# Last stage of a fused kernel: scatters ahead of low parts, both tile tables spread over tiles, the last expert's low parts shared between two engines, expert numbers read early, the last product in halves

## The chip, the cores and the metric

One of the eight cores of a Trainium2 chip runs the whole program. The metric is the time on the device in microseconds, the median of several executions. Five engines run their own instruction streams and meet at semaphores: PE (matmuls and transposes), DVE and ACT (vector work), POOL (vector work and the indirect DMAs, which it issues itself) and SP (the other DMAs).

## What is computed

The input x is 4096 tokens (2 sequences of 2048) of 512 features. Four layers are each added to it: cross attention, a quantised feed-forward, a masked cross attention, and at the end a layer of experts. The change is in the last one alone:

```python
def _L1_ffn_ref(x, Wg, bg, We, be):          # x: the layer norm of the residual
    probs = jax.nn.softmax(x @ Wg + bg, axis=-1)         # 512 probabilities a token
    idx = jnp.argmax(probs, axis=-1)
    p = jnp.take_along_axis(probs, idx[..., None], axis=-1)[..., 0]
    e_idx = idx % We.shape[0]                             # 8 experts
    h = jax.nn.relu(jnp.einsum('bsd,edf->besf', x, We) + be[None, :, None, :])
    onehot = jax.nn.one_hot(e_idx, We.shape[0], dtype=x.dtype)
    out = jnp.einsum('besf,bse->bsf', h, onehot) * p[..., None]
    return out
...
x = x + _L1_ffn_ref(_layernorm(x, axis=-1), L1_ffn_Wg, L1_ffn_bg, L1_ffn_We, L1_ffn_be)
```

So each token needs the product with one of eight 512x512 matrices, that of the expert its argmax names, then bias, relu, the factor p, and its own residual row.

## The kernel before

The expert stage is the class ExpertStage. It walks over tiles of 128 tokens with one running number t. Tiles 0 to 31 are gate tiles, in the order of the tokens, and four of them make a group (0 to 7). Tiles 32 to 70 are the 39 product tiles, j = t - 32, of rows that have been sorted by expert. The gate tiles 0 to 3 belong to the end of the attention stage; from t = 4 on every engine runs a loop `rest` of its own over t, and the order of the calls in that loop is the order on the engine.

A tile passes through the engines like this. ACT's `norm(t)` (L2516) writes the normalised tile. PE's `turn(t)` transposes it (four matmuls, L2766). ACT's `take_hi(t)` (L2523) copies the transposed tile out rounded, and DVE's `take_lo(t)` (L2587) takes what the rounding left. PE multiplies both parts with the two parts of a weight: three matmuls for each of four 128-row pieces k. In gate tiles this is `logits(t)` (L2776 to L2778); in product tiles `product(j)` (L2819 to L2821), whose expert is read from a table into a register. In its iteration t PE does `turn(t + 1)`, then the matmuls of t. Of what it multiplies the low parts of the expert weights are made by POOL (`weights_low`, L2468) from the loaded weights and from their high parts, which ACT casts (`weights_high`, L2535). The high parts of expert e >= 2 are written over the residual rows of group e - 2, so they wait until those rows have been scattered.

In gate tiles DVE finds the largest logit and its index (`top`, L2596 to L2601), ACT sums the exponentials (L2529). After each group DVE makes the one-hots (`hot`, L2606 to L2613), PE ranks the rows within their experts by small matmuls (`rank_rows`, L2789 to L2799), DVE turns the ranks into places (`places`, L2618 to L2628), and POOL scatters the four tiles of residual rows to these places in DRAM (`scatter_rows`, L2477).

Each expert's region in DRAM is rounded to whole tiles, in two steps. After six groups (EARLY = 6) an early count tells of 17 tiles (FULL_TILES) that are certainly full, and after all eight a late count places the other 22 (REST_TILES). Each step is a chain of small DVE instructions: `tile_count` (L2633 to L2641), `tile_ends` (L2646 to L2652), `early_ends` or `late_ends`, and `tile_table` (L2662 to L2675), which writes `tile_expert` and `tile_row`. The early chain stands at t = 25, 26 and 27, the late one at t = 34, 35 and 36. `no_row` (t = 33) and `rows_behind` (t = 34) prepare filler rows, which SP writes behind each expert's last row and at the end (nine DMAs), the first ahead of load 8 and one behind each of loads 8 to 15.

SP loads the sorted rows of product tile j into one of eight buffers (`load`, L2418). Load 0 waits for the early table and six scattered groups, load 4 for seven groups, load 17 for the late table, all groups and all filler rows; from load 8 on each waits until tile j - 8 is finished. In product tiles DVE adds the bias (`add_bias`, L2713, which first reads the expert's number), and in `finish` takes relu and factor (L2719) and adds the residual (L2721) into one of four y buffers; POOL scatters this to the output (`scatter_out`, L2484). The next use of the buffer waits for that DMA.

In POOL's loop two low parts of expert e stand ahead of the scatter of group e - 1 and two behind it, and waits on `out_full` and `hot_ready` hold the low parts back to set times. Of expert 7, pieces 0 and 1 wait until PE has done tile 28, pieces 2 and 3 until DVE has made the last one-hots, in its iteration t = 32. Product 0 waits for the low parts of expert 7 piece by piece.

## Time and profile before

| what | value |
|---|---|
| runs (three) | 1486.5, 1483.89, 1485.26 us; median 1485.26 |
| profiled execution | 1482.94 us |
| its span | 1481.1 us, so 1.8 us lie around it |
| mean granted clock of TensorE | 0.988 |
| busy share of the span | PE 96%, DVE 81%, ACT 58%, POOL 35% |
| expert stage, tiles 4 to 70 | transposes of tile 4 at 1234.24, last matmul near 1469.5 |
| DVE busy, 1370 to 1463 us | 73.6 of 93 us |
| last indirect DMA issued | 1472.60 |

A line of a timeline gives start and duration in microseconds, engine, line of the kernel, operation, what is written from what, and how many instructions the line merges. In square brackets stands how long the engine had been idle before it, and which instruction released it. Matmul durations overlap, so the distance between starts is what counts. PEclk is the clock that TensorE was granted, as a share of 2.4 GHz.

### The profile page before, as it was taken

Reading aid. Unit: us, or ns where it says so; the run is one execution under the profiler, and the core shown is the slowest. Engines: PE = TensorE matmul, PEld = TensorE weight load, DVE = VectorE, ACT = ScalarE, POOL = GpSimd, SP = SyncE. Lnnn points to the kernel's source line nnn. Section 1 sums busy time; section 2 is a strip of 40 time slices with the busy share of each in tenths; the row PEclk is TensorE's granted clock in tenths of the full one; section 3 lists DMA queues with packets and bytes.
Section 4 is the critical chain, followed back from the end, with each engine's and each line's share of the span. In section 5 each row is a group of like instructions: output and inputs, shape, how many; then the busy total and the mean of one; then the engine's idle time right before and its main releaser. Section 6 shows DMA issues by size and latency. Waiting matters only on the chain. (4 is left out here: it accounts for less than half of the span.)

```text
span 1481.1 us, 30113 instructions
## 1 busy us (share of the span) xinstructions
PE 1420.4 (96%) x10457; PEld 1065.1 (72%) x10478; DVE 1198.1 (81%) x2580; ACT 864.1 (58%) x2056; POOL 523.6 (35%) x507
## 2 busy tenths in 40 slices
PE   7999999999999999899998999999999989998996
PEld 5777777777777777644443467888888877776885
DVE  6778787887878765699988968999999986787775
ACT  2544444444444444655548747999999876773432
POOL 0122222222222222200004646655656655664333
PEclk9999999999999999999999999999999999999998
DMA  8511111110111102235507610000000025226641
GB/s 302 185 47 46 46 46 46 46 42 8 37 39 40 46 8 79 47 107 185 184 16 287 246 42 2 4 2 3 3 4 4 4 87 209 98 94 200 193 152 57
DMA packets 68658, 122.03 MB, mean 82 GB/s; under 512 B 30398, under 2 KB 36926, under 8 KB 67008
## 3 DMA queue, kind: packets, MB, share of 16 engines
q1 hardware_dynamic: 62864, 103.71, 20.7%
q0 software_dynamic: 5680, 16.85, 2.9%
q8 instruction: 66, 1.08, 0.3%
q14 instruction: 48, 0.39, 0.1%
HBM read 77.46 MB, written 39.80 MB: 79 GB/s over the span
## 5 line engine op out<-in xcount | busy, mean ns | idle before, releaser
L1835 ACT ACTIVATE c_probs<-c_score,c_minus_top 128x128 f32<-128x128 f32 x512 | 181.2, 381 | 27.9 <-DVE c_minus_top L1981 25.7
L1778 POOL TENSOR_TENSOR c_probs<-c_probs,c_recip 128x512 f32<-128x512 f32 x128 | 140.8, 1103 | 131.2 <-DVE c_recip L1991 127.5
L700 POOL TENSOR_TENSOR a_attn_lo_parts<-a_attn,a_attn_hi_parts 128x512 fp32r<-128x512 f32 x64 | 80.6, 1291 | 200.5 <-ACT a_attn_hi_parts L762 200.5
L758 ACT COPY a_attn<-a_pv_ps 128x512 f32<-128x512 f32 x64 | 36.6, 572 | 145.3 <-PE a_pv_ps L1068 145.3
L1451 POOL TENSOR_TENSOR xres<-xres,b_delta 128x512 f32<-128x512 f32 x24 | 48.3, 2028 | 196.9 <-DVE b_delta L1508 196.9
L1835 ACT ACTIVATION_READ_ACCUMULATOR c_probs<-c_score,c_minus_top 128x1 f32 x512 | 112.8, 220 | 0.0
L430 PE MATMUL a_bank<-a_x_hi_parts,a_wq_hi 128*128 128x256 f32 x512 | 106.5, 289 | 0.3 <-PEq L445 0.3
L696 POOL TENSOR_TENSOR a_x_lo_parts<-a_x_full,a_x_hi_parts 128x512 fp32r<-128x512 f32 x30 | 38.0, 1289 | 192.9 <-ACT a_x_hi_parts L733 192.9
L430 PE MATMUL a_bank<-a_x_lo_parts,a_wq_hi 128*128 128x256 f32 x512 | 102.4, 281 | 0.0
L430 PE MATMUL a_bank<-a_x_hi_parts,a_wq_lo 128*128 128x256 f32 x512 | 102.3, 281 | 0.0
L727 ACT ACTIVATE a_x_full<-a_bank,a_shift,a_gain 128x256 f32<-128x256 f32 x60 | 30.2, 555 | 119.4 <-PE a_bank L422 119.4
L1036 PE MATMUL a_bank<-a_wo_hi,a_attn_hi_parts 128*128 128x512 f32 x248 | 99.4, 401 | 0.0
L1038 PE MATMUL a_bank<-a_wo_hi,a_attn_lo_parts 128*128 128x512 f32 x248 | 98.1, 396 | 0.0
L1037 PE MATMUL a_bank<-a_wo_lo,a_attn_hi_parts 128*128 128x512 f32 x248 | 98.0, 395 | 0.0
L2523 ACT CAST d_xT_hi<-c_score 128x512 fp32r<-128x512 f32 x67 | 39.3, 587 | 97.9 <-PE c_score L2766 92.1
L1304 ACT ACTIVATE b_silu<-b_gate,ahead_scale 128x512 f32<-128x512 f32 x88 | 60.2, 684 | 61.7 <-PE b_gate L1380 61.1
L742 ACT ACTIVATE a_probs<-a_score_ps 128x1024 f32<-128x1024 f32 x64 | 65.6, 1025 | 41.2 <-PE a_score_ps L1053 41.2
L1975 DVE COPY_PREDICATED_SCALAR c_score<-c_masks,c_tiny 128x512 f32 (+1 forms) x96 | 89.1, 928 | 0.0
L1380 PE MATMUL b_up<-b_xT,ahead_upT 128*128 128x512 bf16 x342 | 88.5, 379 | 0.3
L1380 PE MATMUL b_gate<-b_xT,ahead_gateT 128*128 128x512 bf16 x340 | 88.2, 379 | 0.4
L430 PEld LDWEIGHTS a_bank<-a_x_hi_parts,a_wq_hi 128*128 128x128 f32 x512 | 78.3, 188 | 14.2 <-issue 6.3
L1981 DVE TENSOR_REDUCE c_minus_top<-c_score 128x4 f32<-128x512 f32 (+1 forms) x96 | 83.4, 869 | 3.3
(352 smaller groups left out, 4244.3 us busy)
## 6 DMA issues: line engine op xcount, KB each, us to landing
hidden<-b_hidden SPq DMA_DIRECT2D x5, 2816.0 KB, 8.3
b_hidden<-hidden SPq DMA_DIRECT2D x5, 2816.0 KB, 11.4
xres<-in_x SPq DMA_DIRECT2D x8, 1024.0 KB, 14.4
d_we<-in_we SPq DMA_DIRECT2D x8, 1024.0 KB, 6.5
xres<-in_w_gate_up SPq DMA_DIRECT2D x7, 1024.0 KB, 5.3
d_got<-rows SPq DMA_DIRECT2D x20, 258.0 KB, 2.8
xres<-rows SPq DMA_DIRECT2D x19, 258.0 KB, 2.6
a_rot<-in_rot SPq DMA_DIRECT2D x16, 256.0 KB, 3.0
```

Source lines behind the costliest of these rows:

```text
L430: last = nc.tensor.matmul(out[:, i, :], w[:, k, cols], x[:, k, :], start=(j == 0 and i == 0), stop=(j == len(products) - 1 and i == 1))
L700: nc.gpsimd.tensor_tensor(of_spread(attn_lo, g), of_spread(attn, g), of_spread(attn_hi, g), ALU.subtract).then_inc(attn_lo_ready, 1)
L742: nc.scalar.activation(buf, score_ps[:, p % 2], ACT.Tanh, scale=1.0 / (DH0 ** 0.5 * GROK)).then_inc(capped, 1)
L1036: nc.tensor.matmul(out, hi, w_hi, start=first, stop=False)
L1037: nc.tensor.matmul(out, hi, w_lo, start=False, stop=False)
L1038: return nc.tensor.matmul(out, lo, w_hi, start=False, stop=last)
L1304: nc.scalar.activation(silu[:, u % RING, :], gate_ps[:, u % RING, :], ACT.Silu, scale=gate_scale[:, i:i + 1]).then_inc(silu_ready, 1)
L1380: last = nc.tensor.matmul(ps[:, u % RING, :], w[:, k, i * P:(i + 1) * P], xT[:, n % 2, k, :], start=(k == 0), stop=(k == KB - 1))
L1778: nc.gpsimd.tensor_tensor(part, part, recip[:, t % 2, heads].unsqueeze(2).to_broadcast([P, QUADS, KEYS]), ALU.mult).then_inc(scaled, 1)
L1835: last = nc.scalar.activation(probs[:, t, at, :], score_ps[:, h, g, :], ACT.Exp, bias=minus_top[:, h, g:g + 1], accum_out=total[:, t, at:a ...
L1975: ch.step(nc.vector.copy_predicated(part, masks[:, j, t, :].unsqueeze(1).to_broadcast(shape), tiny[:].unsqueeze(2).to_broadcast(shape)))
L1981: nc.vector.tensor_reduce(minus_top[:, PIECES[i]].rearrange("p h g -> p (h g)"), part, AX.X, ALU.max, negate=True).then_inc(top_ready, 1)
```

## The change

In POOL's loop the scatter of group e - 1 comes first and all four low parts of expert e behind it; of expert 7 POOL makes only pieces 0 and 1, then scatters group 6. Group 7 is scattered two tiles at a time behind the first two outputs. DVE makes pieces 2 and 3 of expert 7 at t = 31 (`last_low`). ACT's casts for group 2 stand at t = 10 and 11 (two each) in place of 9, 10, 11; those of expert 7 at t = 29 and 30. The early chain has fewer steps, and its first table step stands a tile earlier; of `early_ends` four steps go to t = 34. The late chain is spread over t = 34 to 39. DVE reads an expert's number at the end of the tile before. SP writes the nine filler rows at loads 11 to 14 (FILL = 11). The last product, its bias and its finish are done in two halves of 256 columns.

```diff
+        FILL = G + 3
+        LAST_SLOT, HALVES = SLOT_TILES - 1, (slice(0, D // 2), slice(D // 2, D))
         def pieces(t):
+            if t // TPC == 2:
+                return {0: (), 1: (), 2: (0, 1), 3: (2, 3)}[t % TPC]
             return {0: (), 1: (0, 1), 2: (2,), 3: (3,)}[t % TPC]
...
-                sp.wait_ge(no_row_set, 2)
-                sp.dma_start(io["rows"][NO_ROW:NO_ROW + P, :], no_token[:]).then_inc(filled, 16)
-                sp.wait_ge(behind_ready, 1)
                 for j in range(G, SLOT_TILES):
                     load(j)
-                    if j - G < EXPERTS:
-                        first = sp.value_load(behind_u[0:1, j - G:j - G + 1], min_val=0, max_val=NO_ROW - P)
-                        sp.dma_start(io["rows"][bass.ds(first, P), :], no_token[:]).then_inc(filled, 16)
+                    if j == FILL:
+                        sp.wait_ge(no_row_set, 2)
+                        sp.dma_start(io["rows"][NO_ROW:NO_ROW + P, :], no_token[:]).then_inc(filled, 16)
+                        sp.wait_ge(behind_ready, 1)
+                    for e in range(2 * (j - FILL), 2 * (j - FILL) + 2):
+                        if 0 <= e < EXPERTS:
+                            first = sp.value_load(behind_u[0:1, e:e + 1], min_val=0, max_val=NO_ROW - P)
+                            sp.dma_start(io["rows"][bass.ds(first, P), :], no_token[:]).then_inc(filled, 16)
...
             def weights_low(e, k):
                 pool.wait_ge(we_hi_ready, KB * e + k + 1)
-                if e >= 1 and k < 2:
+                if e >= 1 and k < 2 and e != EARLY:
                     pool.wait_ge(out_full, done(TPC * e))
-                elif e >= 1:
+                elif 1 <= e < EXPERTS - 1:
                     pool.wait_ge(hot_ready, e + 1)
...
-                for e in range(1, EXPERTS):
-                    for k in range(2):
+                for e in range(1, EXPERTS - 1):
+                    scatter_rows(e - 1)
+                    for k in range(KB):
                         weights_low(e, k)
-                    scatter_rows(e - 1)
-                    for k in range(2, KB):
-                        weights_low(e, k)
-                scatter_rows(GROUPS - 1)
+                for k in range(2):
+                    weights_low(EXPERTS - 1, k)
+                scatter_rows(GROUPS - 2)
                 for j in range(SLOT_TILES):
                     scatter_out(j)
+                    if j < 2:
+                        scatter_rows(GROUPS - 1, range(2 * j, 2 * j + 2))
...
                     if t < GATES:
-                        for k in pieces(t):
+                        for k in pieces(t) if t < GATES - 2 else ((2, 3), ())[t - GATES + 2]:
                             weights_high(t // TPC, k)
...
-                ch.step(nc.vector.tensor_copy(counts[:], counted(i)))
-                ch.wait()
-                ch.step(nc.vector.tensor_scalar(whole[:], counts[:], float(add), None, ALU.add))
-                ch.wait()
-                ch.step(nc.vector.tensor_copy(whole_i[:], whole[:]))
+                ch.step(nc.vector.tensor_scalar(whole_i[:], counted(i), float(add), None, ALU.add))
...
+            def last_low():
+                for k in range(2, KB):
+                    at = EXPERTS - 1, k
+                    dve.wait_ge(we_hi_ready, KB * EXPERTS - KB + k + 1)
+                    nc.vector.tensor_tensor(we_lo[:, at[0], k], we[:, at[0], k], we_hi[:, at[0], k], ALU.subtract).then_inc(constants, 1)
...
                     if t > GATES:
-                        add_bias(t - GATES - 1)
+                        add_bias(t - GATES - 1, number)
...
                         finish(t - GATES - 1)
+                    if t >= GATES:
+                        number = expert_number(t - GATES)
...
                     if t == TPC * EARLY + 2:
                         early_ends()
+                        tile_passed(FULL_TILES)
                     if t == TPC * EARLY + 3:
-                        tile_table(0, FULL_TILES)
-                    if t == GATES + 1:
+                        tile_experts(0, FULL_TILES)
+                        tile_rows(0, FULL_TILES)
+                    if t == GATES - 1:
+                        last_low()
+                    if t == GATES + 2:
+                        early_taken()
+                    if t == GATES + 3:
                         no_row()
-                    if t == GATES + 2:
+                    if t == GATES + 4:
                         tile_count(1, P - 1)
                         rows_behind()
-                    if t == GATES + 3:
+                    if t == GATES + 5:
                         late_ends()
-                    if t == GATES + 4:
-                        tile_table(FULL_TILES, REST_TILES)
-                add_bias(SLOT_TILES - 1)
-                finish(SLOT_TILES - 1)
+                    if t == GATES + 6:
+                        tile_passed(REST_TILES)
+                        tile_experts(FULL_TILES, REST_TILES)
+                    if t == GATES + 7:
+                        tile_rows(FULL_TILES, REST_TILES)
+                for half in range(len(HALVES)):
+                    add_bias(LAST_SLOT, number, half)
+                    finish(LAST_SLOT, half)
...
+                for half, cols in enumerate(HALVES if j == LAST_SLOT else (slice(0, D),)):
+                    if half == 1:
+                        out = logit_place(t + 1)
+                        pe.wait_ge(y_used, j - RING + 2)
+                    for k in range(KB):
+                        if j == 0 and k >= 2:
+                            pe.wait_ge(constants, CONSTANTS + k - 1)
+                        elif j == 0:
+                            pe.wait_ge(we_lo_ready, KB * (EXPERTS - 1) + k + 1)
```

Left out are: `tile_passed`, `tile_experts` and `tile_rows`, which are `tile_table` in three parts, with its last casts folded into the instruction before (9 instructions become 7); `early_taken`, the last four steps of `early_ends`; `rows_behind`, one instruction in place of two; and `add_bias`, `finish` and the matmuls with the columns of their half.

## Rows read from the trace of the kernel before

**Rows 1.** PE timeline: start, duration, instruction; tiles 41 and 70 begin

```profile
1370.10 0.60 PE L2766 MATMUL c_score<-ident,c_xn 128*128 128x128 f32 x4
...
1463.47 0.60 PE L2766 MATMUL c_score<-ident,c_xn 128*128 128x128 f32 x4
```

**Rows 2.** PE timeline: tiles 11 and 12 begin

```profile
1260.79 0.60 PE L2766 MATMUL c_score<-ident,c_xn 128*128 128x128 f32 x4
...
1264.93 0.66 PE L2766 MATMUL c_score<-ident,c_xn 128*128 128x128 f32 x4 [0.77 <-ACT c_xn L2516]
```

**Rows 3.** PE timeline: tiles 28 (first row) and 30 (last row) begin

```profile
1317.43 0.60 PE L2766 MATMUL c_score<-ident,c_xn 128*128 128x128 f32 x4
...
1319.26 0.50 PE L2776 MATMUL c_score<-d_wg_hi,d_xT_hi 128*128 128x512 f32 x1 [1.23 <-DVE d_xT_lo L2587]
...
1326.63 0.19 PE L2789 MATMUL c_bank<-d_base,d_ones 128*128 128x32 bf16 x1 [0.91 <-DVE d_onehot L2613]
...
1326.79 0.64 PE L2766 MATMUL c_score<-ident,c_xn 128*128 128x128 f32 x4
```

**Rows 4.** PE timeline: tiles 33 (first row) and 35 (last row) begin

```profile
1336.54 0.60 PE L2766 MATMUL c_score<-ident,c_xn 128*128 128x128 f32 x4
...
1340.48 0.50 PE L2819 MATMUL c_bank<-d_we_hi,d_xT_hi 128*128 x1 [1.96 <-POOL d_we_lo L2468]
...
1342.54 0.22 PE L2789 MATMUL c_bank<-d_base,d_ones 128*128 128x32 bf16 x1
...
1347.55 0.60 PE L2766 MATMUL c_score<-ident,c_xn 128*128 128x128 f32 x4
```

**Rows 5.** windows: stretch, length, busy (x) PE PEld DVE ACT POOL, PEclk, DMA, GB/s

```profile
1342.00:1346.00 4.00, 4.00 (x24) 3.22 (x24) 2.04 (x5) 1.30 (x2) 0.00 (x0) 0.57 0.81 230
```

**Rows 6.** PE timeline: tiles 37 and 38 begin; product 6

```profile
1353.96 0.60 PE L2766 MATMUL c_score<-ident,c_xn 128*128 128x128 f32 x4
...
1358.42 0.66 PE L2766 MATMUL c_score<-ident,c_xn 128*128 128x128 f32 x4 [0.79 <-ACT c_xn L2516]
...
1364.00 0.49 PE L2819 MATMUL c_score<-d_we_hi,d_xT_hi 128*128 x1 [0.99 <-DVE d_xT_lo L2587]
```

**Rows 7.** ACT timeline: casts of tile 9, copy of tile 37

```profile
1262.54 1.14 ACT L2535 CAST d_we_hi<-d_we 128x512 fp32r<-128x512 f32 x2 [2.38 <-DMA rows<-xres,d_slot_u]
...
1357.07 0.59 ACT L2523 CAST d_xT_hi<-c_score 128x512 fp32r<-128x512 f32 x1 [4.38 <-remote]
```

**Rows 8.** DVE timeline: early count (two rows), late count

```profile
1314.28 1.22 DVE L2637 CAST d_whole_i<-d_whole 128x8 int32<-128x8 f32 x1
1315.53 1.22 DVE L2639 TENSOR_SCALAR d_whole_i<-d_whole_i 128x8 int32<-128x8 int32 x1
...
1351.20 0.17 DVE L2637 CAST d_whole_i<-d_whole 128x8 int32<-128x8 f32 x1
```

**Rows 9.** POOL timeline: two low parts of expert 5

```profile
1314.18 2.54 POOL L2468 TENSOR_TENSOR d_we_lo<-d_we,d_we_hi 128x512 fp32r<-128x512 f32 x2 [1.65 <-ACT d_we_hi L2535]
```

**Rows 10.** line L2477, row scatters: ns min/median/max, first and last start

```profile
L2477 POOL DMA_INDIRECT rows<-xres,d_slot_u x32: 956/961/1238, 1250.5 to 1351.3; - x32
```

**Rows 11.** DVE timeline: a gate tile without extras begins (tile 22's largest logit)

```profile
1304.43 0.70 DVE L2596 CUSTOM_DVE_ANT_0 c_score<-c_score,router_bg 128x512 f32<-128x512 f32 x1 [1.01 <-PE c_score L2778]
```

**Rows 12.** DVE timeline: bias and residual of the last tile

```profile
1469.85 0.69 DVE L2713 TENSOR_TENSOR d_y<-c_score,d_be 128x512 f32<-128x512 f32 x1 [0.83 <-PE c_score L2821]
...
1471.10 0.69 DVE L2721 TENSOR_TENSOR d_y<-d_y,xres 128x512 f32<-128x512 f32 x1
```

**Rows 13.** SP timeline: a filler row, three issues later a load

```profile
1358.59 0.36 SPq L2431 DMA_DIRECT2D rows<-router_bg  x1
...
1362.19 0.33 SPq L2418 DMA_DIRECT2D d_got<-rows  x1
```

**Rows 14.** PE timeline: 256-column matmuls of the attention stage

```profile
1108.89 0.28 PE L2137 MATMUL c_bank<-c_x_lo_parts,c_wq_hi 128*128 128x256 f32 x1
1109.01 0.28 PE L2138 MATMUL c_bank<-c_x_hi_parts,c_wq_lo 128*128 128x256 f32 x1
```

More of the change, by code:

```diff
@@ L2343, in __init__ @@
         slot, slot_u = sb("slot", [P, TPC]), sb("slot_u", [P, TILES], U32)
-        counts, whole_i, whole = sb("counts", [P, EXPERTS]), sb("whole_i", [P, EXPERTS], I32), sb("whole", [P, EXPERTS])
-        behind, behind_u = sb("behind", [1, EXPERTS]), sb("behind_u", [1, EXPERTS], U32)
+        whole_i, whole = sb("whole_i", [P, EXPERTS], I32), sb("whole", [P, EXPERTS])
+        behind_u = sb("behind_u", [1, EXPERTS], U32)
         ends, start = sb("ends", [1, EXPERTS]), sb("start", [1, EXPERTS])
@@ L2475, in scatter_rows @@
                 hold()
-                for t in range(TPC * g, TPC * (g + 1)):
+                for t in range(TPC * g + tiles.start, TPC * g + tiles.stop):
                     nc.gpsimd.indirect_dma_start(out=io["rows"], out_offset=bass.IndirectOffsetOnAxis(ap=slot_u[:, t:t + 1], axis=0),
@@ L2668, in tile_table, with tile_rows @@
+            def tile_rows(j0, n):
                 ch.step(nc.vector.tensor_reduce(row_of[:, 0:n], jumps[:, 0:n], AX.X, ALU.add))
                 ch.wait()
-                ch.step(nc.vector.scalar_tensor_tensor(row_of[:, 0:n], row_of[:, 0:n], origin[:, 0:1], place, ALU.add, ALU.add))
-                ch.step(nc.vector.tensor_copy(tile_expert[:, j0:j0 + n], expert_of[:, 0:n]))
+                ch.step(nc.vector.scalar_tensor_tensor(row_of[:, 0:n], row_of[:, 0:n], origin[:, 0:1], ahead.table("slot", 1)[:, 0:n], ALU.add, ALU.add))
@@ L2672, in tile_table, with early_ends, early_taken @@
                 ch.wait()
-                ch.step(nc.vector.tensor_scalar(row_of[:, 0:n], row_of[:, 0:n], float(NO_ROW), None, ALU.min))
+                nc.vector.tensor_scalar(tile_row[:, j0:j0 + n], row_of[:, 0:n], float(NO_ROW), None, ALU.min).then_inc(tables_ready, 1)
+            def early_ends():
+                tile_ends(whole[0:1], ahead.table("first_row", 1))
+            def early_taken():
+                first = ahead.table("first_row", 1)
                 ch.wait()
-                nc.vector.tensor_copy(tile_row[:, j0:j0 + n], row_of[:, 0:n]).then_inc(tables_ready, 1)
@@ L2677, in early_ends @@
-            def early_ends():
-                first = ahead.table("first_row", 1)
-                tile_ends(whole[0:1], first)
                 ch.step(nc.vector.tensor_scalar(taken[:], start[:], -1.0, float(P * FULL_TILES), ALU.mult, ALU.add))
@@ L2689, in late_ends @@
             def late_ends():
+                ch.wait()
                 ch.step(nc.vector.tensor_tensor(left[:], whole[0:1], taken[:], ALU.subtract))
@@ L2694, in rows_behind @@
             def rows_behind():
-                ch.step(nc.vector.tensor_tensor(behind[:], counts[0:1], ahead.table("first_row", 1), ALU.add))
-                ch.wait()
-                nc.vector.tensor_copy(behind_u[:], behind[:]).then_inc(behind_ready, 1)
+                nc.vector.tensor_tensor(behind_u[:], counted(1)[0:1], ahead.table("first_row", 1), ALU.add).then_inc(behind_ready, 1)
             def no_row():
@@ L2708, in add_bias, with expert_number @@
+            def expert_number(j):
+                return dve.value_load(tile_expert[0:1, j:j + 1], min_val=0, max_val=EXPERTS - 1)
+            def add_bias(j, number, half=0):
+                b, cols = j % Y, HALVES[half] if j == LAST_SLOT else slice(0, D)
                 if j == 0:
                     dve.wait_ge(ld_be, 16)
-                if j >= Y:
+                if j >= Y and half == 0:
                     dve.wait_ge(stored[b], 16 * (j // Y))
-                dve.wait_ge(out_full, done(GATES + j))
@@ L2713, in add_bias @@
-                nc.vector.tensor_tensor(y[:, b, :], logit_place(GATES + j), be[:, number, :], ALU.add).then_inc(y_used, 1)
-            def finish(j):
-                b, u = j % Y, j % G
-                ch.step(nc.vector.tensor_copy(token_u[:, b:b + 1], got[u][:, COL_TOKEN:COL_TOKEN + 1]))
-                dve.wait_ge(y_used, j + 1)
-                ch.step(nc.vector.tensor_scalar(y[:, b, :], y[:, b, :], 0.0, got[u][:, COL_P:COL_P + 1], ALU.max, ALU.mult))
+                dve.wait_ge(out_full, done(GATES + j) + half)
@@ new lines, in add_bias, with finish @@
+                nc.vector.tensor_tensor(y[:, b, cols], logit_place(GATES + j + half)[:, cols], be[:, number, cols], ALU.add).then_inc(y_used, 1)
+            def finish(j, half=0):
+                b, u, cols = j % Y, j % G, HALVES[half] if j == LAST_SLOT else slice(0, D)
+                if half == 0:
+                    ch.step(nc.vector.tensor_copy(token_u[:, b:b + 1], got[u][:, COL_TOKEN:COL_TOKEN + 1]))
+                dve.wait_ge(y_used, j + half + 1)
+                ch.step(nc.vector.tensor_scalar(y[:, b, cols], y[:, b, cols], 0.0, got[u][:, COL_P:COL_P + 1], ALU.max, ALU.mult))
```

35 lines of the change are left out of this document (15 added, 20 removed).

## The prediction

> **What bounds the kernel now.** I read the slices of the page first: PE is busy in 9 tenths of nearly every slice, and from 1240 us on the expert stage runs. Then the PE timeline of that stage, where each tile begins with four transposes (L2766), so the distance between two such starts is the price of a tile. From tile 41 to tile 70 they stand (1463.47 - 1370.10) / 29 = 3.22 us apart and PE has no gap [rows 1]: there TensorE is the bound, and nothing that the other engines save counts. So the change can only win where a tile took longer than 3.22 us. I looked for those places and found four, between tile 11 (1260.79) and tile 41 (1370.10).
>
> Gap 1, tiles 11 to 12: 4.14 us, so 0.92 lost [rows 2]. ACT waited 2.38 us for the scatter of group 0 to land before its cast L2535 could overwrite those rows [rows 7], and so normalised the next tile late.
> Gap 2, tiles 28 to 30: 9.36 us for two tiles and the rank matmuls of a group (0.16, from 1326.63 to 1326.79), which cost 6.60 undisturbed: 2.76 lost [rows 3]. The releasers are the low parts and the one-hots of DVE.
> Gap 3, tiles 33 to 35: 11.01 us against 6.44 for two tiles and 0.3 for ranks and counts: 4.27 lost [rows 4]. PE waited 1.96 for POOL's low parts of expert 7 and 0.28 more for the last of them; afterwards its granted clock was 0.57 over 4 us [rows 5], a mix of its two levels, 1.2 and 2.4 GHz, having been 1.00 before. The remaining 2.0 is that.
> Gap 4, tiles 37 to 41: 16.14 us for four tiles, 12.88 undisturbed: 3.26 lost [rows 1, 6], first behind ACT's normalised tile, then behind DVE's low part.
> Sum 11.2 us: with PE the bound on both sides, the ceiling of all that the change does before the last tile.
>
> **The parts.**
> Scatters first, and group 2's casts at tiles 10 and 11 in place of 9, 10, 11. POOL's order was two low parts, scatter, two low parts. Two low parts are 2.54 us [rows 9], so each scatter goes out some 2.5 us earlier than now (group 0's first DMA starts at 1250.5 [rows 10]). Four DMAs take POOL 4 x 0.96 [rows 10], some 5 us with what lies between them. The low parts come behind it, 5 us later than before, but PE reads none until tile 32. And ACT asks for the landing one tile, over 3 us, later. The old landing let ACT go on at 1262.54; in tile 10 the casts stand behind the copy of the transposes of 1260.79, a norm and the exponentials, so not before 1263, and find even that done. Gain 0.9, between 0 (SP's large loads share the DMA engines here) and 0.92. ACT then has two tiles with a copy of 0.59, two casts of 1.14 [rows 7], a norm and the exponentials of some 0.8 each: 3.0 to 3.3 us with and without their overlaps, about the 3.22 of a tile. I take 0.9.
>
> Early count and table. At tile 25 DVE ran five small instructions, of which two took 1.22 us each; the same cast took 0.17 at 1351.20 [rows 8]. Both long ones end within 0.05 us of the ends of POOL's two subtractions of 1314.18 to 1316.72 [rows 9]: DVE was held out for as long as POOL ran. In the new order POOL is scattering at that moment (from about 1313.7 for 5 us), and the count is three instructions: 0.6 us in place of 3.1. The ends lose four instructions to tile 34 (0.8 us moves), the table loses two casts and the first step moves a tile forward. In a gate tile without extras DVE waits 1.01 us for PE [rows 11]: that is the room. By my schedule the extras at tiles 25, 26 and 27 are 3, 5 and 6 small instructions, 0.6, 1.0 and 1.3 us. Gain 2.76 less what a new lock costs. Bounds: 1.5 and 2.76. I take 2.6.
>
> Last expert's low parts. Parts 2 and 3 of expert 7 leave POOL, where they began only after the last one-hots, and stand on DVE at tile 31, before top(31). Two SBUF subtractions of 128x512 cost 0.69 each by L2721 [rows 12], some 1.3 together, in a tile with 1 us of room: top(31), the one-hots, the exponentials and the norm of tile 34 go back by 0.3 to 0.6. They need ACT's cast of part 3, now one tile earlier, behind a full ACT tile (3.0 us). PE's 2.24 us of waiting goes; what is late next is that norm, 0.4 us. With no wait of 2 us the clock should stay, which gives back the 2.0. Gain 4.27 - 0.4 = 3.9; the lower bound is 1.5, if a wait as long as the old one is left in another place and only part of it goes.
>
> Late tables spread over tiles 34 to 39, and expert numbers read early. DVE in a product tile works some 2.5 us (three passes of 0.69 [rows 12] and two short ones) and had 7, 5 and 9 small instructions more in tiles 34, 35 and 36, at 0.2 each (0.17 [rows 8] and the step to the next) 1.4, 1.0 and 1.8 or more. Each add of the bias read its expert's number just before. Now the extras of tiles 34 to 39 are 4, 2 (two memsets, one of them wide), 4, 5, 4 and 3 instructions, 0.6 to 1.1 us a tile, so DVE is a little over 3.22 in some of them and recovers later; PE uses a low part only one tile after it is made. The number is read behind finish, where DVE's own work covers it. Scattering the last group two tiles at a time lets the first output go 2.5 us earlier, so the four y buffers come free no later. But the first of the losses begins with ACT: an idle of 4.38 us up to 1357.07 whose releaser the trace cannot name [rows 7], though the transposes it needs were out by 1354.5. Nothing in the change removes that, unless it was the traffic of the last scatter and the filler rows. Bounds 0 and 3.26; nearest is the upper one, since two of the three losses are DVE's. I take 2.7.
>
> SP: the nine filler rows move from loads 8 to 15 into loads 11 to 14. SP issues come 1.2 us apart (three steps from 1358.59 to 1362.19) [rows 13], so 13 issues take 15.6 us in place of 4 x 3.22 = 12.9. The loads run four to five tiles ahead; 2.7 us late costs nothing.
>
> Last product in halves. 256-column matmuls start 0.12 us apart [rows 14], so 24 of them take 2.88 against 2.77 of twelve wide ones: 0.1 lost. The chain on DVE from 1469.85 to 1471.79 [rows 12] is halved, but the previous tile and the first half keep DVE busy until about 1470.3. I work out an end at 1471.5. Gain 0.3; bounds -0.1 (halves no faster) and 0.7.
>
> Sum 0.9 + 2.6 + 3.9 + 2.7 + 0.3 = 10.4. The profiled execution took 1482.94 us (span 1481.1), so 1472.5 by its own time. The median of the three runs is 2.3 above that, 1485.26, and the forecast against it is **1474.8 us**.
>
> **A rule against this change.** What rows show is that a cast and a tensor_scalar of DVE stood still while POOL subtracted [rows 8, 9]; no row shows a DVE subtraction with both inputs in SBUF meeting one. The Trainium skill (SBUF — State Buffer, section "Who interferes with whom") states that such an instruction, too, is shut out by a GpSimd instruction that reads SBUF, whole instruction by whole instruction. The trace agrees for the casts; by that rule the two new subtractions can be held as well. The rival below carries it.
>
> **The rivals.**
> 1. DVE and POOL meet in a new place. POOL's parts of experts 6 and 7 are now six subtractions in a row, 7.6 us from the one-hots of tile 28 [rows 9], straight over places(6) and up to last_low at tile 31. Held twice or three times by 1.22 us [rows 8], DVE comes 2.5 to 3.7 late to tile 32, PE waits again and the clock falls again: gap 3 gives 0 to 1 instead of 3.9, gap 2 0.5 less. Gain 6.5: 1478.8. For: the room of 1 us a tile. Against: ends near 1331, last_low near 1333. Chance 0.20.
> 2. The losses at tiles 37 to 41 are ACT's unnamed stall and the traffic of the scatters, not the tables. They stay or move: gain 7.7, 1477.6. Chance 0.13.
> 3. Slower: SP. The nine fillers go into four loads. If reading a number and issuing cost 2.5 us instead of 1.2, thirteen issues take 32 us. The loads' lead is about 4.5 tiles less 3 us of landing, 11 us. Then loads 15 and 16 come 32 - 12.9 - 11 = 8 us late, PE idles that long, and its clock falls once or twice (2 each): 12 lost against 10.4 won, 1486.9. It decides from (12.9 + 11) / 13 = 1.8 us an issue. Against: 1.2 in the same traffic [rows 13]. Chance 0.03.
> 4. It does not do what it says: the waits are replaced one for one and the gain is under 3 us. For: the orders of all five engines change at once. Chance 0.04.
> The forecast itself (gain 8.5 to 11.5) has 0.60.
>
> **How the numbers follow.** A measurement of this kernel tells about 0.2% (3 us) from no change. Faster by more than that: 0.60 + 0.20 + 0.13 = 0.93; within: 0.04; slower 0.03. Low end: 1485.26 - 11.2 - 0.7 = 1473.4, less 1.3 for the spread of three runs: 1472.0. High end: rivals 1 and 2 together leave 3.8, 1481.5; with a chance of 0.03 for both, 1480.0 keeps the range at 8 in 10.
>
> **What would show it.** Right: tile distances of 3.22 to 3.3 from 11 to 12, 28 to 30 and 33 to 41; the granted clock 1.0 around tile 34; no 1.22 us cast; the last chain on DVE ending 0.3 us sooner after the last matmul's old end. Wrong: a DVE subtraction or cast over 1 us between tiles 28 and 31, a clock under 1 after tile 32, an ACT idle with no releaser near tile 37, loads landing after ACT wants them at tiles 45 to 48.

## The result, and the profile after

| | kernel before | changed kernel |
|---|---|---|
| first comparison, six runs each | median 1484.83 us (1483.26 to 1486.5) | median 1477.65 us (1476.54 to 1478.35) |
| ratio | | 0.9949, 95% interval 0.9939 to 0.9959 |
| profiled execution | 1482.94, span 1481.1 | 1477.26, span 1475.5 |
| mean granted clock | 0.988 | 0.99 |

Faster by 7.2 us between medians (0.5%, more than the 0.2% that can be told from no change), 5.7 between the two profiled executions. The forecast was 1474.8 in a range of 1472.0 to 1480.0: inside the range, but 3 us of the expected 10.4 are missing. Where they went is the matter of this part.

PE timeline of the changed kernel, as in [rows 1 to 4, 6]; the transposes of a tile are now L2793, the first matmul of a product L2852. Tiles 13, 14, then 28, 29, 30, then 33, 34, 35, then 37, 38, 39 begin here:

```profile
1267.99 0.60 PE L2793 MATMUL c_score<-ident,c_xn 128*128 128x128 f32 x4
1272.40 0.19 PE L2816 MATMUL c_bank<-d_base,d_ones 128*128 128x32 bf16 x1 [1.02 <-DVE d_onehot L2622]
1272.57 0.64 PE L2793 MATMUL c_score<-ident,c_xn 128*128 128x128 f32 x4
...
1318.45 0.60 PE L2793 MATMUL c_score<-ident,c_xn 128*128 128x128 f32 x4
1321.66 0.60 PE L2793 MATMUL c_score<-ident,c_xn 128*128 128x128 f32 x4
1325.04 0.64 PE L2793 MATMUL c_score<-ident,c_xn 128*128 128x128 f32 x4
...
1334.72 0.60 PE L2793 MATMUL c_score<-ident,c_xn 128*128 128x128 f32 x4
...
1338.35 0.66 PE L2793 MATMUL c_score<-ident,c_xn 128*128 128x128 f32 x4
1339.26 0.50 PE L2852 MATMUL c_bank<-d_we_hi,d_xT_hi 128*128 x1 [0.26 <-issue]
1342.14 0.60 PE L2793 MATMUL c_score<-ident,c_xn 128*128 128x128 f32 x4
...
1348.57 0.60 PE L2793 MATMUL c_score<-ident,c_xn 128*128 128x128 f32 x4
1353.85 0.66 PE L2793 MATMUL c_score<-ident,c_xn 128*128 128x128 f32 x4 [1.89 <-ACT c_xn L2525]
...
1357.61 0.60 PE L2793 MATMUL c_score<-ident,c_xn 128*128 128x128 f32 x4
```

From tile 28 to 30 the two tiles take 6.59 us where [rows 3] had 9.36. From 33 to 35 they take 7.42 instead of 11.01, with no wait for a low part and, in the windows of the same stretch (columns as in [rows 5]: stretch, length, busy PE, PEld, DVE, ACT, POOL, PEclk, DMA share, GB/s), at full clock:

```profile
1338.00:1342.00 4.00, 3.74 (x28) 2.99 (x28) 3.08 (x9) 1.59 (x3) 0.19 (x1) 1.00 0.30 102
1342.00:1346.00 4.00, 4.00 (x23) 3.33 (x22) 3.33 (x11) 1.32 (x3) 3.18 (x4) 1.00 0.83 235
```

But tile 13 takes 4.58 us, which it did not before, and tiles 37 and 38 take 5.28 and 3.76. All gaps in one table, for this and for every later profile: the time lost between the beginnings of two tiles, that is their distance less 3.22 us a tile and less the small matmuls in it (0.16 in 28 to 30, 0.3 in 33 to 35, 0.22 in 13 to 15, as before has it).

| profile | time | tile 4 begins | 11-12 | 13-15 | 28-30 | 33-35 | 37-43 | tile 70 to the end |
|---|---|---|---|---|---|---|---|---|
| before | 1482.94 | 1234.24 | 0.92 | 0.0 | 2.76 | 4.27 | 3.28 | 17.63 |
| before, again (f2) | 1485.66 | 1236.55 | 1.18 | 0.0 | 2.75 | 4.25 | 3.52 | 17.61 |
| changed | 1477.26 | 1235.02 | 0.0 | 1.23 | 0.0 | 0.68 | **3.11** | 17.48 |
| changed, again (f1) | 1475.33 | 1235.71 | 0.0 | 1.26 | 0.0 | 0.64 | 0.66 | 17.40 |
| changed, again (g1) | 1477.89 | 1235.74 | 0.0 | 1.03 | 0.0 | 0.65 | **3.37** | 17.45 |
| e1 | 1475.91 | 1235.92 | 0.0 | 1.34 | 0.0 | 0.67 | 0.92 | 17.43 |
| e2 | 1474.06 | 1233.63 | 0.0 | 1.24 | 0.0 | 0.66 | 1.48 | 17.48 |
| e3, low parts of expert 2 later | 1473.80 | 1235.69 | 0.0 | 0.0 | 0.0 | 0.65 | 0.37 | 17.44 |
| g2, the same again | 1475.69 | 1233.68 | 0.0 | 0.0 | 0.0 | 0.69 | **4.25** | 17.46 |
| e4, POOL makes all of expert 7 | 1476.92 | 1233.80 | 0.0 | 1.41 | 0.0 | 4.42 | 0.16 | 17.42 |
| f3, late tables together | 1476.67 | 1236.47 | 0.0 | 1.15 | 0.0 | 0.64 | 1.35 | 17.46 |
| g3, f3 and the number read late | 1478.70 | 1236.63 | 0.0 | 1.14 | 0.0 | 0.70 | 3.16 | 17.44 |
| f4, group 7 scattered in one piece | 1474.36 | 1233.69 | 0.0 | 1.57 | 0.0 | 0.65 | 1.40 | 17.48 |
| g4, old order on POOL, last product whole | 1476.94 | 1234.62 | 0.0 | 0.0 | 0.43 | 0.51 | **4.05** | 17.60 |

Bold figures are executions of the changed kernel and its variants with a stall at tile 37, an idle of 5.2 to 5.4 us on ACT, told of below. The names e1 to g4 stand for the experiments of the next section. Tile 4 begins anywhere from 1233.6 to 1236.6, in work that the change does not touch: that alone spreads single executions over 3 us, so edits are read from their own column and not from the total.

First profile against first profile: 0.9 - 1.2 + 2.8 + 3.6 + 0.2 + 0.15 = 6.4 won, 0.8 lost ahead of tile 4, in all the 5.6 us by which the spans differ.

**Tile 13.** POOL timeline, then DVE timeline, of the changed kernel:

```profile
1263.87 0.19 POOL L2467 TENSOR_TENSOR d_held<-d_held 128x1 f32<-128x1 f32 x1 [3.90 <-DMA rows<-xres,d_slot_u]
...
1269.35 2.53 POOL L2475 TENSOR_TENSOR d_we_lo<-d_we,d_we_hi 128x512 fp32r<-128x512 f32 x2
```

```profile
1269.79 2.13 DVE L2615 TENSOR_SCALAR d_expert_i<-d_where 128x4 uint32<-128x4 uint32 x1
1271.95 0.17 DVE L2617 CAST d_expert<-d_expert_i 128x4 f32<-128x4 uint32 x1
1272.15 0.19 DVE L2622 TENSOR_TENSOR d_onehot<-router_tables,d_expert 128x32 bf16<-128x32 f32 x1
```

The scatter of group 1 now stands ahead of the low parts and waits 3.90 us for group 0's rows to land, so the low parts of expert 2 run from 1269.35 to 1271.88 (they began at 1263.24 in before), exactly when DVE makes the one-hots of group 2. A tensor_scalar on 4 numbers a partition takes 2.13 us (0.17 in other groups) and ends 0.04 us behind POOL's pair. PE waits 1.02 us for the one-hots. Such a meeting of DVE and POOL is what the change took away at tile 25; here is one at tile 12. I call it the lock.

**Tile 37.** Timeline of ACT and of DVE in the first profile of the changed kernel:

```profile
1352.50 0.59 ACT L2532 CAST d_xT_hi<-c_score 128x512 fp32r<-128x512 f32 x1 [5.21 <-remote]
```

```profile
1350.08 0.06 DVE L2709 MEMSET router_bg<- 128x1 f32 x1
1351.86 0.69 DVE L2727 TENSOR_TENSOR d_y<-c_score,d_be 128x512 f32<-128x512 f32 x1 [1.72 <-remote]
```

It answers to the second of [rows 7]. The releaser has no name again (`remote`). PE had issued the transposes of tile 37 at 1348.57, so ACT's copy was due at 1349.2.

### The profile page after: what moved, and what is told of

It is laid out like the page before. It is cut to its first block and busy times, and to the rows that moved or that the text cites. A ratio compares the mean times of both kernels' runs of the same rounds, so it can differ in the third digit from the quotient of the medians.

```text
span 1475.5 us, 30161 instructions
## 1 busy us (share of the span) xinstructions
PE 1419.7 (96%) x10490; PEld 1065.0 (72%) x10490; DVE 1199.3 (81%) x2576; ACT 865.4 (59%) x2056; POOL 523.0 (35%) x506
```

## The experiments

The kernels ran in three groups of four; those of a group shared a chip, and each group had another one.

**First group: e1 to e4.** Is the stall at tile 37 tied to a place in ACT's program? e1 and e2 put small copies into ACT's gate tiles and change nothing else, e1 five in each of tiles 8, 12, ... 28, e2 five in 24 and 28.

```diff
+                    if t % TPC == 0 and 8 <= t <= 28:      # e2: 24 <= t <= 28
+                        for i in range(5 * (t - 8) // TPC, 5 * (t - 8) // TPC + 5):
+                            nc.scalar.copy(pad[:, i:i + 1], total[:, t - 3:t - 2])
```

> Edit: thirty one-element ACT copies (0.2 us each) into a scratch column, five in each of the gate tiles 8, 12, ... 28, where ACT has 1.4 us of room. Nothing else. Theory A (the ACT idle of 5.2 us with no releaser before the copy of tile 37 is tied to a position in ACT's own instruction stream, where its next instructions have to be fetched): with thirty instructions more ahead of it the idle leaves tile 37 for a place some 8 to 15 tiles earlier, where DMA traffic is lower and it is shorter; tile 37 to 38 takes 3.2 to 3.4 us in place of 5.28, and the run is 2 to 2.6 us faster than the changed kernel, about 1475.3. Theory B (it is a wait of that moment: DMA traffic of loads, scatters and outputs, or a semaphore that comes late): the idle stays before tile 37, tile 37 to 38 stays at 5.0 to 5.4, time 1477 to 1478.

> Edit: the same copies, but only ten, in the gate tiles 24 and 28. Theory A: the unnamed ACT idle moves by ten instructions, two to five tiles earlier than tile 37, so to tiles 32 to 35, and is still there with a length over 2 us beyond what the tile needs. Theory B: it stays before tile 37 with some 5 us.

e1: 1476.09 us median of four (before 1485.83; ratio 0.9935, 0.9918 to 0.9951). e2: 1474.06 in one run. Neither has the stall: tiles 37 and 38 stand 3.2 us apart. That would have been a proof, had not e3 and e4, with ACT's stream as it was, lost the stall as well. So these two runs prove nothing about ACT.

e3 holds the first low parts of expert 2 back until the one-hots of group 2 are made:

```diff
-                if e >= 1 and k < 2 and e != EARLY:
+                if e >= 1 and k < 2 and e not in (2, EARLY):
```

> Edit: low parts 0 and 1 of expert 2 on POOL wait for the one-hots of group 2 (tile 12) as pieces 2 and 3 do, in place of the end of tile 8. Theory: the new loss at tiles 13 to 14 (4.58 us, of it PE 1.02 behind the one-hots) comes from DVE's first step of the one-hots, held 2.13 us by these two subtractions, which ran late because the scatter ahead of them waited 3.9 us for the landing of group 0. Then tile 13 to 14 goes to 3.4 and the run is 1.2 us faster than the changed kernel (about 1476.4), though two DVE steps at tile 13 may be held by up to 1.2 us without cost for PE. Rival (the loss is DVE's own place in the queue, PE or the copies of ACT, which now has two casts in tiles 10 and 11): the one-hots stay late, tile 13 to 14 over 4 us, time 1477.6.

1474.10 us median of four (1473.8 to 1475.57), ratio 0.9924 (0.9908 to 0.9941). DVE timeline, then POOL timeline:

```profile
1270.46 0.17 DVE L2615 TENSOR_SCALAR d_expert_i<-d_where 128x4 uint32<-128x4 uint32 x1
```

```profile
1271.21 5.03 POOL L2475 TENSOR_TENSOR d_we_lo<-d_we,d_we_hi 128x512 fp32r<-128x512 f32 x4 [1.26 <-DVE d_onehot L2622]
```

The same instruction takes 0.17 again, and the loss at tiles 13 to 15 goes from 1.23 to 0. The lock is shown to be its whole cause.

e4 gives parts 2 and 3 of expert 7 back to POOL:

```diff
-                elif 1 <= e < EXPERTS - 1:
+                elif e >= 1:
                     pool.wait_ge(hot_ready, e + 1)
...
                 scatter_rows(GROUPS - 2)
+                for k in range(2, KB):
+                    weights_low(EXPERTS - 1, k)
...
-                    if t == GATES - 1:
-                        last_low()
```

> Edit: of the change only the sharing of expert 7 is undone: pieces 2 and 3 are made by POOL behind the scatter of group 6 and after the last one-hots, none on DVE. Theory: the sharing is what closed the third gap: tiles 33 to 35 go from 7.4 us back to 10 to 11 (PE waits 2 to 3 us for the low parts and its granted clock falls afterwards), 3 to 4 us slower than the changed kernel. Rival (the early order of POOL, not the sharing, closed it): the wait stays under 1 us and the loss under 1 us.

1476.92 us. PE timeline, and the window at 1338:

```profile
1337.78 0.50 PE L2850 MATMUL c_bank<-d_we_hi,d_xT_hi 128*128 x1 [1.98 <-POOL d_we_lo L2475]
1339.03 0.79 PE L2850 MATMUL c_bank<-d_we_hi,d_xT_hi 128*128 x1 [0.30 <-POOL d_we_lo L2475]
```

```profile
1338.00:1342.00 4.00, 3.70 (x22) 2.67 (x22) 0.69 (x1) 0.04 (x1) 0.89 (x1) 0.63 0.44 117
```

Both halves of gap 3 are back, 2.28 us of waiting and a clock of 0.63 behind it; the loss is 4.42 against 0.67. The sharing is worth 3.75 us in this execution: 2.3 are the wait, and the other 1.5 stand beside the lower clock behind it.

**Second group: f1 to f4.** f1 and f2 are the two kernels unchanged, to see whether the stall belongs to the program or to the execution.

> The changed kernel, unchanged, profiled once more. In its first profile ACT was idle for 5.21 us up to 1352.50 (its copy of tile 37, releaser not named) and tiles 37 and 38 were 5.28 and 3.76 us apart. If the program's own order makes that stall, it is here again, within 0.3 us, and tiles 37 to 41 lose some 3 us. If it is a matter of the single execution, it is gone, tiles 37 and 38 stand 3.22 us apart, and the span is some 2.5 us shorter (near 1473). The loss of 1.2 us at tile 13 must be here in both cases.

> The kernel before, unchanged, profiled once more. Its first profile had ACT idle for 4.38 us up to 1357.07 at tile 37. If the order of the work makes the stall, it is here again; if it is a matter of the single execution, it may be gone, and then tiles 37 and 38 stand 3.2 to 3.4 us apart, and the span is up to 2 us shorter than 1481.1. The losses at tiles 11, 28, 29, 33 and 34 (0.92, 2.76 and 4.27 us in sum) must be here within 0.4 us.

f1 took 1475.33 us, f2 1485.66, and f1's ACT timeline at tile 37 reads:

```profile
1349.83 0.59 ACT L2532 CAST d_xT_hi<-c_score 128x512 fp32r<-128x512 f32 x1 [1.92 <-PE c_score L2793]
```

So the same program runs with the stall and without it. The kernel before without it (PE timeline, tiles 37 to 40 begin):

```profile
1356.43 0.60 PE L2766 MATMUL c_score<-ident,c_xn 128*128 128x128 f32 x4
1357.24 0.50 PE L2819 MATMUL c_bank<-d_we_hi,d_xT_hi 128*128 x1 [0.20 <-DVE d_xT_lo L2587]
1360.13 0.60 PE L2766 MATMUL c_score<-ident,c_xn 128*128 128x128 f32 x4
1361.37 0.50 PE L2819 MATMUL c_bank<-d_we_hi,d_xT_hi 128*128 x1 [0.65 <-DVE d_xT_lo L2587]
1364.26 0.60 PE L2766 MATMUL c_score<-ident,c_xn 128*128 128x128 f32 x4
1366.72 0.50 PE L2819 MATMUL c_score<-d_we_hi,d_xT_hi 128*128 x1 [1.86 <-DVE d_xT_lo L2587]
1369.60 0.60 PE L2766 MATMUL c_score<-ident,c_xn 128*128 128x128 f32 x4
```

It loses 3.5 us all the same, every one behind DVE's low part. So in before the stall added nothing: with it gap 4 costs 3.28, without it 3.52. In the changed kernel, whose DVE is no longer late, the stall stands open: 3.11 and 3.37 with it, 0.66 without. In this pair, with no stall on either side, the change won 10.3 us: 0.8 ahead of tile 4 by chance, 0.2 in the tail and 9.25 between (1.2 - 1.3 + 2.75 + 3.6 + 2.9, and 0.1 elsewhere).

f3 puts the late tables together again, at t = 33 to 36 as before:

```diff
-                    if t == GATES + 2:
+                    if t == GATES + 1:
                         early_taken()
-                    if t == GATES + 3:
                         no_row()
-                    if t == GATES + 4:
+                    if t == GATES + 2:
                         tile_count(1, P - 1)
                         rows_behind()
-                    if t == GATES + 5:
+                    if t == GATES + 3:
                         late_ends()
-                    if t == GATES + 6:
+                    if t == GATES + 4:
                         tile_passed(REST_TILES)
                         tile_experts(FULL_TILES, REST_TILES)
-                    if t == GATES + 7:
                         tile_rows(FULL_TILES, REST_TILES)
```

> The changed kernel with the late count, ends and table put together again as before: the four steps left from the early ends with no_row at t = 33, count at 34, ends at 35, all of the table at 36. If spreading them is worth something, DVE comes late at tiles 35 to 38: they lose 0.5 to 2.5 us more than in the changed kernel without its stall (tiles 34 and 37 to 41 then lose more than 0.6 and 2.0 in sum). If the loss there was never DVE's tables, the tiles from 34 to 41 lose no more than in the changed kernel and the time is 1474 to 1478. If the lost time at 37 was ACT's, an idle of over 4 us at tile 37 stands in ACT's timeline or does not, whatever the tables do.

1476.67 us, no stall, 1.35 lost in tiles 37 to 43 against 0.66 in f1. Its one PE row with a wait stands in the product behind the tables:

```profile
1357.93 0.52 PE L2850 MATMUL c_score<-d_we_hi,d_xT_hi 128*128 x1 [1.03 <-DVE d_xT_lo L2596]
```

Tile 39 alone loses 1.33 here and at most 0.05 in the six executions with spread tables and no stall (f1, e1 to e4, f4). But these six lose 0.16 to 1.48 in the whole column, most of it at tiles 40 to 42. So spreading moves the loss; that it saves 0.7 is not shown.

f4 scatters group 7 in one piece:

```diff
+                scatter_rows(GROUPS - 1)
                 for j in range(SLOT_TILES):
                     scatter_out(j)
-                    if j < 2:
-                        scatter_rows(GROUPS - 1, range(2 * j, 2 * j + 2))
```

> The changed kernel with all four scatters of group 7 in a row ahead of the first output, as before. The first output goes some 2.5 us later and the traffic of group 7's rows comes in one piece near 1345 to 1350. If the stall at tile 37 hangs on that traffic, it moves or grows; if outputs out late held the y buffers, DVE's add of the bias of product 4 waits for a landed output near tile 37. If neither, this run is like the changed kernel within 1 us, 1474 to 1478.

1474.36 us, no stall, 1.40 lost in tiles 37 to 43 and no wait for an output. Against f1 that is 0.7 more, but e2, which has the split, lost 1.48 there, so a worth of the split is not shown. Whether group 7's traffic has to do with the stall this run can't tell, since no kernel had the stall on this chip.

**Third group: g1 to g4.** g1 is the changed kernel and g2 is e3's edit, both timed more often.

> The changed kernel, unchanged, timed more often. In four profiles without ACT's stall at tile 37 the tiles 37 and 38 stand 3.22 us apart, in the one with it 5.28 and 3.76: 2.6 us. If the stall comes in some executions and not in others, the times fall into a lower part near 1475.3 (the profile without it) and an upper one near 1477.7, and the median lies in one of them; if it had nothing to do with the time, the executions lie around one value. The kernel before should show no such step of 2.6, since there the stall lay over losses that DVE's tables made anyway (3.26 with it, 3.5 without).

> The changed kernel with the low parts 0 and 1 of expert 2 held back until DVE has made the one-hots of group 2, as in the earlier run of this edit, now timed more often beside the unchanged one. The lock at tile 13 is gone (4.6 becomes 3.4), so 1.2 us less than the changed kernel in executions of the same kind: 1474 to 1475 against 1475.3. If its earlier lead of 3.5 us was that alone, the lead is still there; if 2.4 of it was the missing stall at tile 37, the lead is 1.2.

g1: 1477.96 us (1475.92 to 1478.96, five runs) beside 1485.09 for before, ratio 0.9951 (0.9938 to 0.9965). g2: 1476.98 (1475.69 to 1477.79), ratio 0.9945 (0.9932 to 0.9959). g2 leads by 1.0, near the lock's price (1.03 to 1.26 in the changed kernel's own profiles); of the earlier lead of 3.5 the rest fits the stall, which e3's profile lacks. The five times of g1 did not fall into two parts; the 3 us that vary ahead of tile 4 blur a step of 2.5. Both profiles have the stall. All engines' timeline of g1, from the last matmul of product 3 on:

```profile
1348.80 0.40 PE L2854 MATMUL c_score<-d_we_hi,d_xT_lo 128*128 x1
...
1349.04 0.60 PE L2793 MATMUL c_score<-ident,c_xn 128*128 128x128 f32 x4
...
1352.52 0.69 DVE L2727 TENSOR_TENSOR d_y<-c_score,d_be 128x512 f32<-128x512 f32 x1 [2.27 <-remote]
1353.15 0.59 ACT L2532 CAST d_xT_hi<-c_score 128x512 fp32r<-128x512 f32 x1 [5.40 <-remote]
```

Two engines stop, not one. DVE's add needs the signal behind product 3 (`out_full`), ACT's copy the same one and that behind the transposes of tile 37 (`turned`). By PE's records these were due at 1349.2 and 1349.6; the two engines go on at 1352.5 and 1353.15, 3.3 and 3.5 us late and still 0.6 apart, as in the first profile (1351.86 and 1352.50). In g2 they go on together:

```profile
1349.97 0.59 ACT L2532 CAST d_xT_hi<-c_score 128x512 fp32r<-128x512 f32 x1 [5.30 <-remote]
1350.03 0.69 DVE L2727 TENSOR_TENSOR d_y<-c_score,d_be 128x512 f32<-128x512 f32 x1 [2.09 <-PE c_bank L2854]
```

So what they share is PE's signals. The traces also hold the time of each update of a semaphore, and these show the signals themselves late. `turned` is updated 0.61 to 0.71 us behind the start of a tile's transposes nearly everywhere, in every profile. For tile 37 it is updated 3.90, 4.08, 4.00 and 3.98 us behind it in the first profile, g1, g2 and g4, and 3.08 in the first profile of before. The signal of product 3, due 0.17 us behind the same start, comes 3.2 to 3.9 behind it in those four and 2.3 in before. That of product 4 is then only 0.6 to 0.8 late in the four. Whether PE's work itself was late and its records are not, or only the signals, is not shown.

In g2, as in g4, PE's granted clock fell behind the stall, and the loss is about 1 us larger (4.25 and 4.05 against 3.11 and 3.37, where it stayed at 1.00). Window of g2 behind the stall:

```profile
1352.00:1356.00 4.00, 3.83 (x10) 3.04 (x11) 3.73 (x11) 1.30 (x2) 1.34 (x3) 0.61 0.44 93
```

g3 is f3 with the expert's number read just before each add, as before:

```diff
-                        add_bias(t - GATES - 1, number)
+                        add_bias(t - GATES - 1, expert_number(t - GATES - 1))
...
-                    if t >= GATES:
-                        number = expert_number(t - GATES)
```

> The changed kernel with the late tables together at t = 33 to 36 as before and, on top of it, the expert's number read just before each add of the bias. With the tables alone tile 39 lost 1.33 us and tiles 37, 38 nothing, against 0.5, 0.9 and 2.1 in the kernel before. If the early number is worth what is missing, the loss of tiles 35 to 41 grows to 2.5 to 3.5 us. If the shorter count and table are, or POOL's low parts ending earlier, it stays at 1.3 to 1.8. The last tile's chain on DVE gets 0.1 to 0.3 longer in the first case.

1478.70 us, no stall; tiles 37 to 43 lose 3.16 against f3's 1.35, in the same three waits as before:

```profile
1351.09 0.49 PE L2849 MATMUL c_bank<-d_we_hi,d_xT_hi 128*128 x1 [0.43 <-DVE d_xT_lo L2596]
...
1355.10 0.49 PE L2849 MATMUL c_bank<-d_we_hi,d_xT_hi 128*128 x1 [0.53 <-DVE d_xT_lo L2596]
...
1359.98 0.50 PE L2849 MATMUL c_score<-d_we_hi,d_xT_hi 128*128 x1 [1.43 <-DVE d_xT_lo L2596]
```

In front of the adds of products 1, 2 and 3 DVE now sits idle for 0.67, 0.90 and 0.63 us, where f3 has no idle time. The add of product 3 in g3, then in f3:

```profile
1353.67 0.69 DVE L2727 TENSOR_TENSOR d_y<-c_score,d_be 128x512 f32<-128x512 f32 x1 [0.63 <-issue]
```

```profile
1351.90 0.69 DVE L2727 TENSOR_TENSOR d_y<-c_score,d_be 128x512 f32<-128x512 f32 x1
```

Reading the number early is worth 1.8 us in these six tiles, by one execution each. That is more than executions with the early number and no stall differ among themselves (0.16 to 1.48). The tail did not grow (17.44).

g4 has two edits in different places: the old order on POOL, and the last product whole.

```diff
-        LAST_SLOT, HALVES = SLOT_TILES - 1, (slice(0, D // 2), slice(D // 2, D))
+        LAST_SLOT, HALVES = SLOT_TILES - 1, (slice(0, D),)
...
-                if e >= 1 and k < 2 and e != EARLY:
+                if e >= 1 and k < 2:
...
-                    scatter_rows(e - 1)
-                    for k in range(KB):
+                    for k in range(2):
+                        weights_low(e, k)
+                    scatter_rows(e - 1)
+                    for k in range(2, KB):
                         weights_low(e, k)
```

> The changed kernel with two edits that are read at different places. POOL's order for experts 1 to 6 is the old one, two low parts, scatter, two low parts, with the old wait on PE ahead of all first pairs. If the early scatter closed gap 1, tile 11 loses 0.9 again; if the later casts of group 2 did it, tile 11 stays at 3.22, and the lock at tile 13 is gone with it (3.4). At tile 25 the early count meets POOL's pair again: two instructions of DVE take over 1 us, and tiles 28 and 29 lose 1 to 2.8; if the moved table steps closed gap 2, they lose under 0.5. And the last product is whole again: if halves are worth 0.15 to 0.3, the end is 17.6 to 17.8 us behind the transposes of tile 70, against 17.48.

1476.94 us, with the stall. Tile 11 loses nothing with the old order: gap 1 was closed by the casts of group 2 standing a tile later, and the early scatter added only the lock at tile 13, which is gone here. At tile 25 one instruction of DVE meets POOL again (POOL timeline, then DVE's):

```profile
1313.53 2.55 POOL L2475 TENSOR_TENSOR d_we_lo<-d_we,d_we_hi 128x512 fp32r<-128x512 f32 x2 [1.67 <-ACT d_we_hi L2546]
```

```profile
1313.64 1.20 DVE L2648 CAST d_whole<-d_whole_i 128x8 f32<-128x8 int32 x1
```

and tiles 28 to 30 lose 0.43, of 2.76 in before. So the order is 0.4 of gap 2, and 2.3 is what is left of the change in these tiles, above all the shorter and moved count and table, which no run undid alone. The tail is 17.60 whole against 17.40 to 17.48 in halves: 0.15.

## Why the prediction was right, and where it was not

- **Gap 1, "I take 0.9".** The gap closed (0.92 to 0). The step that failed is its reasoning, "the low parts come behind it, 5 us later than before, but PE reads none until tile 32": it asked who needs them and not whom they meet. Nor did it count that the scatter of group 1, now ahead of them, waits for group 0's rows: that wait was 3.90 us, and they ran 6.1 us later. They met the one-hots at tile 12 and cost 1.2, so the term was -0.3. Nor did the early scatter close the gap, as g4 shows, nor land earlier: it let POOL go on at 1263.87, ACT in before went on at 1262.54.
- **Gap 2, 2.6.** Measured 2.76. The three instructions of DVE's count now take 0.16, 0.20 and 0.17 us in place of the 1.22 of [rows 8], as forecast.
- **Gap 3, 3.9.** Measured 3.59. The two subtractions on DVE took 1.28 together (1.3 forecast); the clock stayed at 1.00. Of the 0.68 still lost, 0.41 is at tile 33, as forecast for the norm of tile 34; 0.26 is a wait of PE ahead of product 1 that the sum did not have.
- **Gap 4, "nearest is the upper one, since two of the three losses are DVE's. I take 2.7".** Without the stall that is about what it gives (3.52 to 0.66, 2.9), though 1.8 of it came from the early number, which the step gave two sentences, and none is shown to be the spreading. In the profiled execution it gave 0.2, because a stall that could not be seen in before as a loss of its own came out. The same paragraph says "nothing in the change removes that"; the step then took it as covered, and should have asked what it costs once the cover is gone.
- **Tail, 0.3.** Measured 0.15. The chain on DVE did get shorter, 1.26 us (1464.88 to 1466.14) for the second half against 1.94 in [rows 12]. But it starts 6.86 us behind the transposes of tile 70 against 6.38: the product had ended at 1464.25, and DVE was still busy with the first half. The step had that in it (busy "until about 1470.3"); it came to 8.03 behind the transposes, 8.12 was measured.
- **Rivals.** The first had the right mechanism and the wrong place. At tile 29, where it put it, DVE was held, as the DVE timeline of the changed kernel shows (POOL's six subtractions run from 1324.43 to 1331.97), beside an unhindered row of the same instruction:

```profile
1314.82 0.17 DVE L2637 TENSOR_TENSOR d_carry<-d_carry,d_in_group 128x8 bf16<-128x8 bf16 x1
...
1327.70 0.53 DVE L2633 CAST d_slot_u<-d_slot 128x4 uint32<-128x4 f32 x1
...
1328.38 1.10 DVE L2637 TENSOR_TENSOR d_carry<-d_carry,d_in_group 128x8 bf16<-128x8 bf16 x1
...
1333.97 1.28 DVE L2715 TENSOR_TENSOR d_we_lo<-d_we,d_we_hi 128x512 fp32r<-128x512 f32 x2
```

  It cost DVE 1.3 us and PE nothing, and `last_low` started behind POOL's subtractions, at 1333.97. The held L2637 has both inputs in SBUF. The Trainium skill (SBUF — State Buffer, section "Who interferes with whom") says that a DVE instruction with two SBUF inputs contends with a GpSimd instruction that reads SBUF. The trace agrees, 1.10 us against 0.17. The two new subtractions met none of POOL's, so no run shows them held. The second rival gave 1477.6 and the median came to 1477.65. That the numbers agree is luck: the stall stayed, but tables and number together were worth 2.0 to 3.4 where no stall hid it (3.52 less 0.16 to 1.48), and the lock, which the rival did not have, took 1.2. The third, SP, did not come: from tile 43 to 70 PE loses 0.1 us in sum.
- **Chance.** 0.60 stood on the sum of 10.4, 0.13 on a gain of 7.7, next to which the median came, by another way. In the pair without the stall the gain was 10.3 between single executions, 9.5 counted from tile 4 on.

**Still open.** What holds PE's signals back at tile 37, and why in some executions only. It came in three of four profiles of the third group, in none of eight of the first two, on other chips, and in both first profiles, whose chip is not known. That speaks for the chip; it shows no cause. ACT's stream alone does not make it, since f1 is the same program without it. The recording may have a part: the four profiles of the third group and the two first ones hold 8824 to 8894 updates of semaphores, the eight others 9341 to 9358. But g3 is one of the six, and has no stall at tile 37. From the first group to the third, e3's edit goes from 1474.10 to 1476.98 while before goes from 1485.83 to 1485.09, as with a stall that is covered in before only.

**Best version.** e3's edit, in both comparisons faster than before and, in the one with the changed kernel beside it, 1.0 us under it; the spreads of the two overlap there, but its own column, 1.2 to 0, does not.

## What to carry to other kernels

When a step of a queue is moved, ask not only who waits for it but what it will run beside at the new time: a low part that nobody needed for 20 tiles cost 1.2 us by when it ran. When a stall has no named releaser, profile the kernel before once more ahead of reasoning on it; one that comes and goes is priced by what it costs when its cover is gone. And look for the cheap fixed step in every tile: one register read ahead of an add was worth 1.8 of gap 4, while spreading two chains of small instructions is not shown to be worth anything there.

## What the runs showed that was not expected

- An instruction of DVE on four numbers a partition was held over both of two POOL subtractions in a row, 2.13 us (1.93 to 2.46 in eight other profiles), while at tile 29 the held ones went on after 0.53 and 1.10.
- Two engines that wait for PE's signals can go on 3.3 and 3.5 us later than PE's records would let them, at a full granted clock and with PE's records unbroken for one more product; the updates of the semaphores are as late.
- A wait of PE of 1.98 us was followed by a clock of 0.61 in g2, one of 2.07 in g1 by 1.00, at the same tile of nearly the same program.
- Work ahead of the expert stage that no edit touched ended anywhere within 3 us (tile 4 at 1233.63 to 1236.63).
